# Two-headed attention on one core: sigma scores kept two key tiles deep, tau scores one tile deep

## What is computed

```
S = einsum("bhnd,bhmd->bhnm", Q, K) / dh ** 0.5
W_tau = softmax(S, axis=-1)
W_sigma = 1.0 / ((1.0 + abs(S) / beta) ** 2 + t ** 2)
W_sigma = W_sigma / W_sigma.sum(axis=-1)
f = 0.5 * (W_tau @ V) + 0.5 * (W_sigma @ V)
```

## Time and profile before

| | before |
|---|---|
| median of three runs | 2053.55 us |
| profiled execution's own time | 2050.47 us |
| its span, first to last instruction | 2048.6 us |
| VectorE busy | 1800.0 us, 88% of the span, 3699 instructions |
| ScalarE busy | 1634.4 us, 80%, 1459 instructions |
| TensorE busy | 1571.4 us, 77%, 8452 instructions |
| GpSimd busy | 1419.3 us, 69%, 1070 instructions |
| mean granted TensorE clock | 0.942 of full |
| stages of the heads | from 96.8 us to about 1611 us of the span |

### The profile page before, as it was taken

One profiled execution on the slowest core, in us unless ns is written; L12 is line 12 of the kernel. 1 busy time (PEld: TensorE's weight loads), 2 busy tenths in 40 slices (PEclk: granted clock), 3 DMA queues, 4 the chain that ended last, 5 costly groups with the idle time before them and its releaser, 6 DMA issues. The chain is left out here.

```text
span 2048.6 us, 33898 instructions
## 1 busy us (share of the span) xinstructions
PE 1571.4 (77%) x8452; PEld 572.2 (28%) x8579; DVE 1800.0 (88%) x3699; ACT 1634.4 (80%) x1459; POOL 1419.3 (69%) x1070
## 2 busy tenths in 40 slices
PE   4477777877777777777777778777777587788866
PEld 2212222222222222222222222222221243366655
DVE  5799999999999999999999999999998288755556
ACT  3279999999999999999999999999999311222243
POOL 1398999889998899988999899998998112000010
PEclk9689999999999999999999999999999788877878
DMA  3300000000000000000000000000000000000001
GB/s 106 110 4 15 12 12 12 15 14 12 12 12 15 14 12 12 12 15 14 12 12 13 16 12 12 12 13 16 12 12 6 1 1 0 1 0 0 0 1 41
DMA packets 28862, 31.74 MB, mean 15 GB/s; under 512 B 5209, under 2 KB 16544, under 8 KB 28832
## 3 DMA queue, kind: packets, MB, share of 16 engines
q1 hardware_dynamic: 28832, 31.40, 5.0%
HBM read 22.74 MB, written 8.39 MB: 15 GB/s over the span
## 5 line engine op out<-in xcount | busy, mean ns | idle before, releaser
L860 POOL TENSOR_TENSOR sigma_weights<-grown 128x1024 f32<-128x1024 f32 x448 | 845.7, 1894 | 0.0
L718 DVE TENSOR_SCALAR sigma_weights<-ps_sig 128x512 int32<-128x512 int32 x1024 | 693.2, 677 | 26.5 <-PE ps_sig L617 26.5
L604 PE MATMUL ps_acc<-tau_weights,v_operand 128*9 128x512 f32 x2048 | 529.5, 596 | 134.3 <-ACT sigma_weights L779 134.0
L725 DVE TENSOR_TENSOR running_max<-ps_sig,running_max 128x512 f32<-128x512 f32 x896 | 608.2, 679 | 0.0
L833 POOL TENSOR_SCALAR grown<-sigma_weights,shape_operand 128x1024 f32<-128x1024 f32 x448 | 501.7, 1120 | 139.9 <-DVE sigma_weights L718 139.9
L617 PE MATMUL ps_sig<-q_operand,k_operand 96*128 96x512 bf16 x1024 | 400.2, 391 | 180.3 <-DVE running_max L725 165.2
L604 PE MATMUL ps_acc<-sigma_weights,v_operand 128*9 128x512 f32 x2048 | 531.4, 597 | 0.1
L766 ACT ACTIVATE sigma_weights<-sigma_weights,shape_operand 128x2048 f32<-128x2048 f32 x256 | 508.6, 1987 | 11.2 <-POOL sigma_weights L860 11.2
L807 ACT ACTIVATE tau_weights<-ps_tau 128x1024 f32<-128x1024 f32 x512 | 510.8, 998 | 8.0 <-PE ps_tau L635 8.0
L779 ACT ACTIVATE sigma_weights<-sigma_weights 128x2048 f32<-128x2048 f32 x256 | 484.6, 1893 | 0.0
L635 PE MATMUL ps_tau<-q_operand,k_operand 128*128 128x512 bf16 x897 | 277.8, 379 | 7.9 <-DMA q_operand<-max_rows 0.4
(11 more groups left out here) (172 smaller groups left out, 1511.5 us busy)
## 6 DMA issues: line engine op xcount, KB each, us to landing
q_operand<-q_parts SPq DMA_DIRECT2D x192, 48.0 KB
k_operand<-k_parts SPq DMA_DIRECT2D x64, 144.0 KB
q_parts<-parts SPq DMA_DIRECT2D x12, 256.0 KB, 2.9
k_parts<-parts SPq DMA_DIRECT2D x12, 256.0 KB, 2.9
x_res<-in_L_attn_x SPq DMA_DIRECT2D x4, 512.0 KB, 7.0
q_operand<-max_rows SPq DMA_DIRECT2D x128, 2.0 KB
out<-x_res SPq DMA_DIRECT2D x4, 512.0 KB, 3.2
experts<-in_L_ffn_expert_w SPq DMA_DIRECT2D x1, 512.0 KB
```

Of the source, the lines that this page charges most:

```text
L604: mm = pe.matmul(ps_acc[32 * q:32 * q + COLS, :], vop[:, (slot - 1 + kind) % SLOTS, j, :], weights[:, half * HALF:(half + 1) * HALF], star ...
L718: dve.tensor_scalar(sig[:, tile % SIG_RING, cols].bitcast(I32), ps_sig[:, half, :].bitcast(I32), SIGN_OFF, None, ALU.bitwise_and)\
L725: dve.tensor_tensor(run[:, slot, cols], ps_sig[:, half, :], run[:, slot, cols], ALU.max)\
L860: pool.tensor_tensor(sig[:, tile % SIG_RING, :], t, t, ALU.mult)\
```

## The change

`ps_tau` becomes one buffer of two banks, `ps_sig` two buffers of two banks, one for each of two key tiles. TensorE issues both halves of a sigma tile together, and needs `run_ready` of the tile before the last. VectorE's sign clearing and running maximum each take 1024 columns, two banks, in one instruction: 16 instructions a stage in place of 32. `half_maxima(0)` follows the whole of tile 0, and `half_maxima(1)` the whole of tile 1. TensorE's `turn_running(0)` moves behind `weigh` of step 0, and `turn_running(1)` ahead of the tau tile of step 1. The tau tile waits for `tau_done` of the tile just before it. TAU_SHIFT, MT_STEP and FT_STEP rise by one, so tau tiles, maxima and the turned sums come one step later. The semaphores `sig_ready`, `mag_ready` and `run_ready` count tiles, no longer halves.

```diff
-TAU_SHIFT = 4
+TAU_SHIFT = 5
-MT_STEP, FT_STEP = 1, 3
+MT_STEP, FT_STEP = 2, 4
...
-        ps_tau = ps("ps_tau", [P, 2, 2, HALF])
-        ps_sig = ps("ps_sig", [P, 2, HALF])
+        ps_tau = ps("ps_tau", [P, 2, HALF])
+        ps_sig = ps("ps_sig", [P, 2, 2, HALF])
...
-                    def sigma_scores(half):
-                        wait(pe, run_ready, s * (2 * TB) + (2 * j - 1 + half))
-                        pe.matmul(ps_sig[:, half, :], kop[0:SIGMA_ROWS, slot, keys],
-                                  qop[0:SIGMA_ROWS, slot, half * HALF:(half + 1) * HALF],
-                                  start=True, stop=True).then_inc(sig_ready, 1)
+                    def sigma_scores():
+                        wait(pe, run_ready, s * TB + (j - 1))
+                        for half in range(2):
+                            mm = pe.matmul(ps_sig[:, j % 2, half, :], kop[0:SIGMA_ROWS, slot, keys],
+                                           qop[0:SIGMA_ROWS, slot, half * HALF:(half + 1) * HALF], start=True, stop=True)
+                        mm.then_inc(sig_ready, 1)
...
-                        sigma_scores(0)
-                    elif j == 0 and at(s, NH, NH):
-                        pe.wait_ge(run_ready, 2 * TB * NH)
-                    if j == 0 and at(s, 1, NH):
-                        turn_running((slot - 1) % SLOTS, 0, before)
+                        sigma_scores()
+                    if j == 1 and at(s, 1, NH):
+                        turn_running((slot - 1) % SLOTS, 1, before + 1)
...
-                        wait(pe, tau_done, g - 1)
+                        wait(pe, tau_done, g)
                         for half in range(2):
-                            mm = pe.matmul(ps_tau[:, of % 2, half, :], kop[:, head_slot, of * P:(of + 1) * P],
+                            mm = pe.matmul(ps_tau[:, half, :], kop[:, head_slot, of * P:(of + 1) * P],
...
-                    if at(s, 0, NH - 1):
-                        sigma_scores(1)
...
                         if j == 0:
-                            turn_running((slot - 1) % SLOTS, 1, before + 1)
+                            pe.wait_ge(run_ready, s * TB)
+                            turn_running((slot - 1) % SLOTS, 0, before)
...
-                    def magnitude(half):
-                        dve.wait_ge(sig_ready, s * (2 * TB) + (2 * j + half + 1))
-                        if half == 0:
-                            wait(dve, pv_done, s * TB + (j - SIG_RING + 1))
-                        cols = slice(half * HALF, (half + 1) * HALF)
-                        dve.tensor_scalar(sig[:, tile % SIG_RING, cols].bitcast(I32),
-                                          ps_sig[:, half, :].bitcast(I32), SIGN_OFF, None, ALU.bitwise_and)\
-                           .then_inc(mag_ready, 1)
+                    def magnitude():
+                        dve.wait_ge(sig_ready, s * TB + (j + 1))
+                        wait(dve, pv_done, s * TB + (j - SIG_RING + 1))
+                        scores = ps_sig[:, j % 2, :, :].rearrange("p h q -> p (h q)")
+                        dve.tensor_scalar(sig[:, tile % SIG_RING, :].bitcast(I32), scores.bitcast(I32),
+                                          SIGN_OFF, None, ALU.bitwise_and).then_inc(mag_ready, 1)
...
-                            dve.wait_ge(run_ready, s * (2 * TB) + (2 * j - 1 + half))
-                            dve.tensor_tensor(run[:, slot, cols], ps_sig[:, half, :], run[:, slot, cols], ALU.max)\
-                               .then_inc(run_ready, 1)
-                    if at(s, 0, NH - 1):
-                        magnitude(0)
-                    if j == 0 and at(s, 1, NH):
-                        half_maxima(0, before)
+                            dve.wait_ge(run_ready, s * TB + j)
+                            dve.tensor_tensor(run[:, slot, :], scores, run[:, slot, :], ALU.max).then_inc(run_ready, 1)
...
                     if at(s, 0, NH - 1):
-                        magnitude(1)
+                        magnitude()
+                    if j == FT_STEP + 1 and at(s, 2, NH + 1):
+                        divide(s - 2)
                     if at(s, 1, NH):
-                        if j == 0:
-                            half_maxima(1, before + 1)
+                        if j < 2:
+                            half_maxima(j, before + j)
```

More of the change, by code:

```diff
@@ L711, in stage @@
                         take_sums(s - 1)
-                    def magnitude(half):
-                        dve.wait_ge(sig_ready, s * (2 * TB) + (2 * j + half + 1))
-                        if half == 0:
-                            wait(dve, pv_done, s * TB + (j - SIG_RING + 1))
-                        cols = slice(half * HALF, (half + 1) * HALF)
-                        dve.tensor_scalar(sig[:, tile % SIG_RING, cols].bitcast(I32),
-                                          ps_sig[:, half, :].bitcast(I32), SIGN_OFF, None, ALU.bitwise_and)\
-                           .then_inc(mag_ready, 1)
+                    def magnitude():
[4 more added lines that the diff above has]
+                                          SIGN_OFF, None, ALU.bitwise_and).then_inc(mag_ready, 1)
                         if j == 0:
-                            dve.tensor_copy(run[:, slot, cols], ps_sig[:, half, :]).then_inc(run_ready, 1)
+                            dve.tensor_copy(run[:, slot, :], scores).then_inc(run_ready, 1)
                         else:
-                            dve.wait_ge(run_ready, s * (2 * TB) + (2 * j - 1 + half))
-                            dve.tensor_tensor(run[:, slot, cols], ps_sig[:, half, :], run[:, slot, cols], ALU.max)\
-                               .then_inc(run_ready, 1)
-                    if at(s, 0, NH - 1):
-                        magnitude(0)
-                    if j == 0 and at(s, 1, NH):
-                        half_maxima(0, before)
+                            dve.wait_ge(run_ready, s * TB + j)
+                            dve.tensor_tensor(run[:, slot, :], scores, run[:, slot, :], ALU.max).then_inc(run_ready, 1)
                     sums_use = before + (3 if at(s, 0, NH) else 0)
@@ L737, in stage @@
                     if at(s, 0, NH - 1):
-                        magnitude(1)
+                        magnitude()
+                    if j == FT_STEP + 1 and at(s, 2, NH + 1):
+                        divide(s - 2)
                     if at(s, 1, NH):
-                        if j == 0:
-                            half_maxima(1, before + 1)
+                        if j < 2:
+                            half_maxima(j, before + j)
                         if j == MT_STEP + 1:
                             second_part(s - 1)
-                    if j == FT_STEP + 1 and at(s, 2, NH + 1):
-                        divide(s - 2)
             dve.memset(ps_acc[:, :], 0.0).then_inc(acc_set, 1)
@@ L768, in square_whole @@
             def square_whole(s, slot):
-                act.wait_ge(mag_ready, s * (2 * TB) + (2 * WHOLE + 2))
+                act.wait_ge(mag_ready, s * TB + (WHOLE + 1))
                 act.wait_ge(sqp_ready, pooled(s, 1))
@@ L807, in stage @@
                         act.activation(tau[:, (head_slot * TB + of) % TAU_RING, :],
-                                       ps_tau[:, of % 2, :, :].rearrange("p h q -> p (h q)"),
+                                       ps_tau[:, :, :].rearrange("p h q -> p (h q)"),
                                        ACT.Exp, scale=float(DH) ** -0.5).then_inc(tau_done, 1)
@@ L826, in grow @@
             def grow(s, slot, j):
-                pool.wait_ge(mag_ready, s * (2 * TB) + (2 * j + 2))
+                pool.wait_ge(mag_ready, s * TB + (j + 1))
                 wait(pool, sqp_ready, pooled(s, j - GROWN_RING + 1))
```

## The result

| | before | after |
|---|---|---|
| median of the runs | 2052.85 us (2051.61 to 2053.83, 4 runs) | 2170.73 us (2166.83 to 2173.65, 4 runs) |
| profiled execution's own time, its span | 2050.47, 2048.6 us | 2173.65, 2171.6 us |
| VectorE busy | 1800.0 us | 1710.9 us |
| ScalarE busy | 1634.4 us | 1646.8 us |
| mean granted TensorE clock | 0.942 | 0.89 |

The changed kernel takes 1.0581 of the time of the kernel before (95% interval 1.0568 to 1.0593): 118 us more, where 26 were forecast. The side was right, the size was not, and the result lies outside the range. Two slow executions are left out of all that follows, one of eight of `e3` (7398 us) and one of two of `h1` (2519 us, mean granted clock 0.55).

What follows compares the result with a forecast made beforehand. ScalarE was taken to bound the kernel at 23.21 us a stage. Step 1's 27.9, fill -2.7 and drain +1.3 gave +26.5 on 2050.47, 2077.0; with 3.1 for the median, 2080 us, range 2060 to 2094.

Steps and rivals of the forecast that it cites:

- The side: Whole kernel: the change was forecast to make it slower, chance 0.81.
- ScalarE stays the bound, VectorE's saving is worth nothing: Steady stages: ScalarE sets 23.21 us a stage; VectorE's saving of 1.0 us a stage stays hidden behind it.
- A wide instruction costs 1.13 us and no bank boundary: VectorE's 1024-column instructions: 1.13 us each, bounds 1.12 to 1.19, the upper being two of 512 columns.
- `turn_running(1)` and the whole of tile 0 make the tau tile of step 1 late: Step 1, stages 2 to 63: chain of 5.87 us against 5.42, 0.45 us late, 27.9 us in all.
- the two handovers of 0.09 and 0.04: In step 1's chain: sigma scores from TensorE to VectorE 0.09 us, tau scores from TensorE to ScalarE 0.04.
- One tau buffer is enough elsewhere: Tau tiles at other steps arrive in time, with some 1.0 us left, or 0.6 at odd steps.
- Fill and drain: Start and end of the run: first tau exp stays at 128.91, fill -2.7 us, drain +1.3 us.
- the 1.3 us of the drain: End of the run: tau tiles come one step later, together 17.0 us against 15.7, so +1.3 us.
- the rival on TensorE's clock: TensorE's clock falls to 1.2 GHz, doubling its terms in step 1's chain: 166 us more, 2246 us; chance 0.02.
- the prediction's own signs of being wrong: ScalarE's gaps under 0.1 us a stage, gaps at steps other than step 1, or wide instructions under 1.1 us.
- X: End of ScalarE's exp(-x) of step 6, at 973.58, from which the chain to step 1's tau tile is counted.

Runs made afterwards that it cites:

- e3: The kernel before with one tau buffer in place of two and the wait for the tile just before: 2052.5 us, ratio 1.0010.
- h1: The changed kernel with one extra 64-column VectorE instruction ahead of tile 0's sign clearing, lengthening the stage by 0.13 us: 2116.92 us, one run.
- e5: The changed kernel with the next stage's tile 0 sigma scores ahead of step 7's `weigh` and four unused matmuls behind them: 2050.51 us, ratio 1.0002.
- e1: The changed kernel with six matmuls whose result nobody reads ahead of step 7's `weigh`: 2093.2 us, ratio 1.0213 to the kernel before.
- e4: The changed kernel with the sigma scores of the next stage's tile 0 issued ahead of step 7's `weigh`: 2095.6 us, ratio 1.0225.
- e8: The changed kernel with VectorE's sign clearing and maximum in two instructions of 512 columns each again, same waits: 2105.9 us, ratio 1.0271.
- h2: e8 with one extra 64-column VectorE instruction at tile 0, lengthening the stage by 0.13 us: 2153.6 us, ratio 1.0495.
- g1: e5 with the negated row of maxima moved from ScalarE to VectorE and GpSimd squaring all eight tiles every third stage: 2115.0 us, ratio 1.0296.

## Why the prediction was right and where it failed

- **ScalarE stays the bound, VectorE's saving is worth nothing.** Right, and shown by `e5`: 90 us less of VectorE, the same time. The advice of larger tiles in the Trainium skill, "Advanced Engine Details and Errata", The Read-Write Bubble, which the prediction weighed, holds for the cost of the instruction (1.13 us against twice 0.60), but that engine was not the one that bound.
- **A wide instruction costs 1.13 us and no bank boundary.** Right: 995.67, 996.81, 997.94.
- **`turn_running(1)` and the whole of tile 0 make the tau tile of step 1 late.** Right in place and kind. The term was 0.45 and measured 0.57: the two handovers of 0.09 and 0.04 were 0.13 and 0.12. The sum is within its bounds of 0.38 to 0.61, though the second handover had none of its own. 62 x 0.57 = 35 us, where 27.9 were forecast. `e1` shows what is left when mostly this remains, 2093, at the upper end of the forecast range, and `e4` that it goes when the sigma scores come earlier.
- **One tau buffer is enough elsewhere.** Right at full clock: no gap at other steps in the clean stage, and `e3` showed that the single buffer alone costs nothing.
- **Fill and drain.** The first tau exp stands at 128.91 as forecast, and the fill gave back the 3 us. Of the last ones:

```profile
1714.45 1.00 ACT L798 ACTIVATE tau_weights<-ps_tau 128x1024 f32<-128x1024 f32 x1
1716.31 1.02 ACT L798 ACTIVATE tau_weights<-ps_tau 128x1024 f32<-128x1024 f32 x1 [0.86 <-PE ps_tau L634]
1718.03 1.02 ACT L798 ACTIVATE tau_weights<-ps_tau 128x1024 f32<-128x1024 f32 x1 [0.70 <-PE ps_tau L634]
```

  The tail's tau exps are 1.72 us apart where 1.69 was the least that I gave. But from the exp at 1714.45 to the start of the copy of the last sums, at 1730.08, are 15.6 us as before (15.7), where 17.0 were forecast: the 1.3 us of the drain did not come.
- **The step that failed** is the clock: the sum has no term for it, because the rival on TensorE's clock was set aside with "in which it idled a fifth of the time; now it idles a little more", price "62 x 2.7 = 166 us", chance 0.02. It measured some 78 us (`e1`) to 88 (the account). One of the prediction's own signs of being wrong came true, gaps of ScalarE at another step: 0.91 us at step 0. Two things were wrong in that rival. I looked at the share of idle time, which indeed hardly moved, and not at how it is cut up: the change takes away 309 short waits and leaves one of 2.2 us a stage. That could have been read before, for the prediction itself placed VectorE's old wait and the 0.74 us ahead of `weigh`; it only never added up what TensorE does between the tau tile of step 7 and X. And I took the clock as one level for the whole stretch, so that the rival seemed to be a wild case, while it comes and goes: a few us at a time, in three of four stages, for about half of what the all-or-nothing price said. In the stages of 26.3 us a fall costs 2.5 us, near the 2.7 of that price.

What is shown: the clock falls around the gathered idle piece (the windows), the fall goes in nearly all stages when the piece is filled (`e1`, `e5`), and with fall and chain both gone the loss is nil (`e5`). What is shown as well: the same piece at another stage length often does no harm (`e8`, `h1`, `h2`), and two shorter pieces close together can do it too (`e4`). What stays open: by what rule the chip decides, since four stage lengths are four points and no curve. The Trainium skill, "TensorE: Matmul & The Clock Gate", Part 1, says that the clock follows how busy TensorE has been recently; these runs agree, as every row with a fallen clock shown here stands behind idle time. They add that two kernels with the same piece and close busy shares (77.6% of the stages in the changed kernel, 75.0% in `e8`) can stand 65 us apart.

## What to carry to other kernels

When a change moves work on TensorE, list its waits in order of time and ask where they come to stand close together; fewer and earlier dependencies can gather many harmless waits into a piece that costs the clock. In a loop with an engine at 100%, find for every other engine's instruction how late it may be on that engine's beat, and keep what waits for a reduction (here the second transposes) out of the way of what the full engine wants next. An instruction made wide on an engine with slack saves nothing, and delays by its length whatever follows it in the order. Before work moves to VectorE or GpSimd, look for VectorE instructions with two inputs in SBUF: a short one can be held up for microseconds (0.49 us in `e5`, 3.16 in `g1`).

## What the runs showed that I had not expected

- The granted clock can fall for only a few us and come back, once per stage, in some stages and not in others; 0.13 us more in a stage of 24 us moved the time by 54 us one way and by 48 the other.
- Matmuls that compute nothing made the kernel 78 us faster (`e1`).
- An instruction of 1024 columns on VectorE with two SBUF inputs took 6.22 us beside GpSimd's; those from PSUM took 1.2 beside the same instructions.
